# Pairwise products of embeddings and a tower of three layers: table gathers in short rows between the products, and another split of the reductions

## What is computed

```python
e = jnp.stack([tbl_0[ids[:, 0]], ..., tbl_39[ids[:, 39]]], axis=1)   # 512 x 40 x 64
p = e[:, rowidx]          # first of each pair i < j
q = e[:, colidx]          # second of each pair
z = jnp.einsum('bie,fie,bif->bi', p, param, q)                        # 512 x 780
h = jnp.concatenate([z, dense_ctx], axis=1)                           # 512 x 796
h = jnp.maximum(h @ W_top1 + b_top1, 0.0)                             # 512
h = jnp.maximum(h @ W_top2 + b_top2, 0.0)                             # 256
y = h @ W_top3                                                        # 512 x 1
```

## Time and profile before

| | us |
|---|---|
| median of 3 runs | 548.67 |
| lowest and highest | 548.06, 549.01 |
| the profiled run | 548.24 |
| its span | 546.4 |
| TensorE matmuls busy | 322.2 |
| VectorE busy | 258.1 |
| ScalarE busy | 255.2 |
| GpSimd busy | 185.2 |

### The profile page before, as it was taken

One profiled execution on the slowest core, in us unless ns is written; L12 is line 12 of the kernel. 1 busy time (PEld: TensorE's weight loads), 2 busy tenths in 40 slices (PEclk: granted clock), 3 DMA queues, 4 the chain that ended last, 5 costly groups with the idle time before them and its releaser, 6 DMA issues.

```text
span 546.4 us, 7416 instructions
## 1 busy us (share of the span) xinstructions
PE 322.2 (59%) x2318; PEld 165.8 (30%) x2318; DVE 258.1 (47%) x262; ACT 255.2 (47%) x1961; POOL 185.2 (34%) x192
## 2 busy tenths in 40 slices
PE   0402000220003200299999999899779999999988
PEld 0201000000001000155455544454454344444645
DVE  0000000000000000389899988855437999998590
ACT  1000000000002100389999969734687999995632
POOL 6777777777777760000000000000001122232030
PEclk9998555565555755599999999999889999999999
DMA  2221111211112110174324220032124242420000
GB/s 59 46 50 30 26 26 26 55 26 26 26 25 62 26 26 1 39 268 124 125 89 148 88 95 10 11 92 76 46 95 173 95 143 79 172 95 1 1 2 0
DMA packets 12937, 35.60 MB, mean 65 GB/s; under 512 B 4705, under 2 KB 5985, under 8 KB 11618
## 3 DMA queue, kind: packets, MB, share of 16 engines
q1 hardware_dynamic: 7778, 29.88, 16.4%
q0 software_dynamic: 5120, 5.25, 5.0%
HBM read 35.12 MB, written 0.00 MB: 64 GB/s over the span
## 4 chain that ended last, share of the span: by engine, by line
PE 34%; another core or an unknown queue 24%; issue 19%; ACT 13%; DVE 8%; POOL 1%; DMA 1%; DVEq 0%
ACT prod L658 11%; PE upsum L537 9%; PE upsum L532 7%; DVE prod L622 6%; PE zbank L489 6%; PE abank L444 5%; PE abank L423 1%; DVE z L596 1%; POOL emb L396 1%; PE upsum L501 1%; ACT xT L637 1%; PE upsum L505 1%; PE abank L469 1%; PE upsum L573 1%
## 5 line engine op out<-in xcount | busy, mean ns | idle before, releaser
L658 ACT ACTIVATE prod<-prod 128x64 f32<-128x64 f32 x944 | 227.0, 250 | 8.1 <-issue 7.2
L658 ACT ACTIVATION_READ_ACCUMULATOR prod<-prod 128x1 f32 x944 | 185.3, 196 | 7.7 <-issue 7.7
L396 POOL DMA_INDIRECT emb<-tbl,rows_id x160 | 151.5, 947 | 50.2 <-issue 48.5
L622 DVE TENSOR_TENSOR prod<-upsum,emb 128x1024 f32<-128x1024 f32 x98 | 116.8, 1220 | 107.1 <-remote 68.5
L537 PE MATMUL upsum<-w,xT 64*128 64x512 f32 x392 | 106.0, 641 | 102.3 <-issue 59.1
L405 POOL TENSOR_TENSOR prod<-prod 128x512 f32<-128x512 f32 x26 | 32.9, 1271 | 290.4 <-DVE prod L622 290.4
L622 DVE TENSOR_TENSOR prod<-upsum,xT 128x1024 f32<-128x1024 f32 x82 | 97.7, 1219 | 67.2 <-remote 40.0
L637 ACT ACTIVATE xT<-abank 128x256 f32<-128x256 f32 x40 | 15.1, 378 | 220.1 <-remote 129.3
L532 PE MATMUL upsum<-xT,w 64*128 64x256 f32 x656 | 88.3, 397 | 4.9 <-DVE prod L622 2.6
L537 PEld LDWEIGHTS upsum<-w,xT 64*128 64x128 f32 x392 | 33.8, 191 | 140.3 <-issue 81.2
L532 PEld LDWEIGHTS upsum<-xT,w 64*128 64x128 f32 x656 | 60.3, 190 | 35.9 <-issue 16.8
(11 more groups left out here) (46 smaller groups left out, 132.0 us busy)
## 6 DMA issues: line engine op xcount, KB each, us to landing
w<-W_top SPq DMA_DIRECT2D x2, 1792.0 KB, 8.2
emb<-tbl,rows_id POOLq DMA_INDIRECT x160
w<-param SPq DMA_DIRECT2D x2, 1248.0 KB
w<-param SPq DMA_DIRECT2D x2, 1152.0 KB
w<-param SPq DMA_DIRECT2D x2, 1120.0 KB
w<-param SPq DMA_DIRECT2D x2, 1024.0 KB
w<-param SPq DMA_DIRECT2D x2, 992.0 KB
w<-param SPq DMA_DIRECT2D x2, 896.0 KB
```

Source lines behind the costliest of these rows:

```text
L396: pool.indirect_dma_start(emb[:, c, f, :], None, tables[f], bass.IndirectOffsetOnAxis(ap=rows_id[:, c, f:f + 1].bitcast(U32), axis=0),).th ...
L622: dve.tensor_tensor(to.rearrange("p (h q) -> p h q", h=2), t[:], f.broadcast_to([P, 2, BANK]), ALU.mult).then_inc(multiplied, 1)
L658: last = act.activation(ring[:, x * E:(x + 1) * E], ring[:, x * E:(x + 1) * E], ACT.Copy, accum_out=z_view(u)[:, x:x + 1])
```

## The change

Four things change.

1. GpSimd issues the gathers of the first 10 stretches of half 0 (40 DMAs) at the start, eight at a time: ahead of stretches 2, 4, 6 and 8 it waits until all DMAs of the stretch before have landed (`gathered[0][n - 1]`).
2. The other 120 gathers are placed between the halvings, four per stretch. A stretch's gathers stand at 20 units before its first unit, for half 1's first 10 stretches at unit 22 + 6n. Ahead of each four GpSimd waits until all units before that place are multiplied.
3. The shares: H units are dealt from unit 14 on with 0.25 (before: from unit 112 on with 0.22 and 0.3), V units only up to there. The letters of all 200 units are then T 68, S 62, H 48, V 2, C 20; before T 82, S 59, H 26, V 13, C 20. Of units 0 to 79 26 are T, 27 S, 16 H, 2 V and 9 C.
4. VectorE reduces an H unit 5 units later (H_LAG 3 to 5).

The cuts of the groups of sums follow from the letters: half 0 has 3 turned and 4 flat groups, before 4 and 3. The four parts of layer 1 of half 0 stand at units 105, 108, 111 and 115, before at 104, 107, 111 and 115.

```diff
-H_LAG = 3
+H_LAG = 5
...
+GATHER_FIRST, GATHER_AHEAD, GATHER_OTHER, GATHER_STEP = 10, 20, 22, 6
...
-SHARES = [(0, 0.58, 0.32, 0.1, 0.0), (112, 0.4, 0.3, 0.08, 0.22), (130, 0.4, 0.3, 0.0, 0.3)]
+SHARES = [(0, 0.55, 0.35, 0.1, 0.0), (14, 0.42, 0.33, 0.0, 0.25)]
...
-        return max(u + {"S": S_LAG + 5, "V": V_LAG + 3, "H": H_LAG + 3}[units[u]["by"]] for u in members(s, g))
+        return max(u + {"S": S_LAG + 5, "V": V_LAG + 3, "H": H_LAG + 2}[units[u]["by"]] for u in members(s, g))
...
+    gather_at = {}
+    for q in range(NQ):
+        s, n = stretches[q]["s"], stretches[q]["n"]
+        if s == 0 and n >= GATHER_FIRST or s == 1:
+            at = stretches[q]["first"] - GATHER_AHEAD
+            if s == 1 and n < GATHER_FIRST:
+                at = GATHER_OTHER + GATHER_STEP * n
+            assert at <= stretches[q]["first"] - GATHER_AHEAD
+            gather_at.setdefault(max(at, 0), []).append((s, n))
...
-            for s in range(HALVES):
-                for n in range(NC):
-                    for f in (2 * n, 2 * n + 1):
-                        for c in range(s * PER, (s + 1) * PER):
-                            pool.indirect_dma_start(
-                                emb[:, c, f, :], None, tables[f],
-                                bass.IndirectOffsetOnAxis(ap=rows_id[:, c, f:f + 1].bitcast(U32), axis=0),
-                            ).then_inc(gathered[s][n], 16)
+
+            def gather(s, n):
+                for f in (2 * n, 2 * n + 1):
+                    for c in range(s * PER, (s + 1) * PER):
+                        pool.indirect_dma_start(
+                            emb[:, c, f, :], None, tables[f],
+                            bass.IndirectOffsetOnAxis(ap=rows_id[:, c, f:f + 1].bitcast(U32), axis=0),
+                        ).then_inc(gathered[s][n], 16)
+
+            for n in range(GATHER_FIRST):
+                if n >= 2 and n % 2 == 0:
+
+                    pool.wait_ge(gathered[0][n - 1], 16 * 2 * PER)
+                gather(0, n)
             for u in range(NU):
+                for s, n in gather_at.get(u, []):
+
+                    if u:
+                        pool.wait_ge(multiplied, u)
+                    gather(s, n)
                 if units[u]["by"] == "H":
```

## The result

| | before | changed kernel |
|---|---|---|
| median of 4 runs each | 548.47 | 442.10 |
| lowest and highest | 548.06, 549.01 | 440.98, 442.79 |
| ratio, 95% interval | | 0.8058, 0.8039 to 0.8077 |
| span of the profiled run | 546.4 | 439.2 |

The likeliest value, 399 us, was that of case A ("the stall is gone"). The measured time lies where case B put it ("the stall comes back in parts", 420 to 470 us).

What follows compares the result with a forecast made beforehand. Signals delayed by the 160-gather row bound the start; after the change GpSimd's issue does, to unit 81. Span 546.4 - 153.9 + 2 (clock) + 2 (halvings) = 396.5, plus 1.8 and 0.4: 399 us; range 382 to 460, 8 in 10.

Steps and rivals of the forecast that it cites:

- case A: Whole kernel, the forecast itself: the stall at the start is gone, 385 to 420 us; chance 0.62.
- case B: Gather rows from 49 us on, starting with one of 16: the stall comes back in parts, 420 to 470 us; chance 0.20.
- That the long row of gathers is the stall, and that cutting it is the gain: First 228 us: 160 gathers in one row delay other engines' signals; cutting the row gains 153.9 us at unit 81.
- Debt of 0.15 us a gather: Gather rows: something takes 1.40 us per gather, fed each 1.25; eight owe 1.2 us, which a 1.5 us wait clears.
- GpSimd the bound up to unit 81: Start to unit 81: GpSimd runs without a pause; 116 gathers, 16 halvings and four pauses put unit 81 at 175.7 us.
- The 16 halvings' 20.8 us: GpSimd's first-half halvings at 1.30 us each: 20.8 us on the path while GpSimd is the bound.
- Four pauses at 1.5: First 40 gathers, issued eight at a time: GpSimd's four waits for landing cost 1.5 us each, 6.0 us.
- Rival C: Any gather in flight delays signals, not only long rows: slower than before, about 573 us; chance 0.07.
- From unit 81 on: Units 81 to the end: 216.8 us as before, plus 2 us for halvings late behind four gathers.
- The clock: Up to unit 81: TensorE's lower clock level behind idle gaps adds 2 us to the path, bounds 0 and 10.

Runs made afterwards that it cites:

- changed up to unit 112, nothing held (other chip): Changed kernel with shares T 0.4, S 0.3, H 0.3 from unit 112 on, run where the kernel before took 367.6 us: 396.0 us, ratio 1.077.
- before with spacer: Kernel before with a GpSimd memset of 128 x 256 behind each of its 160 gathers: 506.7 us, ratio 0.9225, where the kernel before took 548.3.
- spacer of 512: Kernel before with a GpSimd memset of 128 x 512 behind each gather, on the chip where the kernel before took 367.6 us: 402.4 us, one run.
- the changed kernel with the spacer: Changed kernel with a memset of 128 x 256 behind each gather, where the kernel before took 367.6 us: 429.0 us, ratio 1.168.

## Why the prediction was right in its range and 43 us off in its value

All terms side by side, in us of the span:

| | unit 81 | from unit 81 on | span |
|---|---|---|---|
| before | 329.6 | 216.8 | 546.4 |
| forecast | 175.7 + 2 | 216.8 + 2 | 396.5 |
| changed kernel | 210.3 | 228.9 | 439.2 |
| changed up to unit 112, nothing held (other chip) | 175.0 | 219.6 | 394.6 |
| old split, pacing only | 225.8 | 225.6 | 451.4 |
| new split, no pacing | 330.5 | 227.3 | 557.8 |
| new split, no gathers | 141.2 | 225.2 | 366.4 |
| old split, plain DMAs | 132.0 | 217.4 | 349.4 |
| before with spacer | 291.3 | 216.7 | 508.0 |
| before with pauses every eight | 286.3 | 217.9 | 504.2 |
| changed, rows of four | 215.2 | 230.8 | 446.0 |

- **That the long row of gathers is the stall, and that cutting it is the gain:** right, and shown from both sides: the new split alone gives no gain, the pacing alone 96 us, and without indirect gathers the stall is gone.
- **Debt of 0.15 us a gather, "so the debt is cleared each time, and I take the stall as gone":** this is the step that failed, and with 33 us in the first part it is most of the miss (210.3 - 177.7). The 1.40 us per gather came from two ends of one stretch, as the text says, and did not fit the text's own row between them: 17 gathers owe 2.6 us by it, and the delay was 14.3. The spacer and the pauses show late signals where it leaves no debt, and in the changed kernel the fourth pause of 1.78 us did not end waits that began at 45.4. The first 45 us went as forecast: four pauses of 1.7 to 2.0 us, and no wait named "remote".
- **GpSimd the bound up to unit 81, 116 x 1.25 + 16 x 1.30 + ...:** the sum is right where nothing is held (175.0 measured), wrong here, since it presumes that the products always run ahead of GpSimd. Here GpSimd waited 32.8 us for them. The 16 halvings' 20.8 us lie on the path only in the first case; here they lay in time that was free anyway. The Trainium skill (GPSIMD Engine Reference, section 4.1, engine selection) puts elementwise adds on VectorE. The pacing with the new split took 442 us, with the old one, which has no halvings in the first half, 452; so with the hold the measurement does not bear the rule out, though no run moves the halvings alone. No run tried the paced kernel without them on the other chip.
- **Four pauses at 1.5:** 1.71, 1.99, 1.73 and 1.78, 7.2 us in place of 6.0. The Trainium skill (DMA: Bandwidth & Descriptors, the anatomy of one DMA on the SWDGE path) gives a fixed cost of some 2.0 us for such a DMA. An estimate from it, counted from the end of issue, is 8.0; the trace lies between.
- **Rival B:** named the right place (the row of 16 from 49 us on) and the right brake ("each delay makes GpSimd wait for products"), at 420 to 470 us with a chance of 0.20. The range held 442 us because it took in B, not because the forecast's path was right. B should have been the larger part: its own evidence, 17 gathers with 14.3 us of delay, was as good as the evidence for A, and the row of 16 stood in the order.
- **Rival C,** "if a row of eight already delays a signal": rows of eight do delay signals. That it gave no slower kernel is because products do run in the gaps that the pacing leaves: GpSimd, waiting for late products, issues nothing. With pauses of only some 2 us between eights and no waits for products it is 494 to 506 us, still under the 548 of one long row.
- **From unit 81 on:** +12.1 where +2 was taken, the second miss, 10 us. Most of it belongs to the new split: the spans of that part are 225 to 231 us in all kernels with it unchanged, also without gathers (225.2) and without pacing (227.3), and 217 to 218 in those with the old split and no waits for products. (With the spacer of 512 it is 239, since its gathers still run then.) Changing the shares from unit 112 on (less S, more H) gave 219.6, on the other chip; there the changed kernel with the spacer took 227.0. By stages 81, 99, 128, 180, 199 and end:

| | 81 to 99 | to 128 | to 180 | to 199 | to the end |
|---|---|---|---|---|---|
| before | 27.9 | 71.3 | 68.4 | 34.7 | 14.6 |
| changed kernel | 25.4 | 71.7 | 72.2 | 40.5 | 19.2 |
| new split, no gathers | 25.0 | 72.0 | 68.4 | 40.8 | 19.1 |
| old split, pacing only | 27.8 | 71.7 | 76.8 | 34.7 | 14.6 |

The change of halves is as it was. The 10 us behind unit 180 stand there without gathers too, so these are the split's. Part of them is one wait of TensorE for ScalarE's copy, 4.0 us, the first row below; all six traces with the unchanged new split have it, those with the old split or with other shares from unit 112 on don't at that place. The 3.8 us from 128 to 180 are gone without gathers, and the old split with pacing alone, 8.8 us over before (225.6 against 216.8), loses 8.4 of them in that stage: both go with the gathers that now stand there. How the gathers cost them isn't shown; little is held there (4.4 us with pacing alone).

That wait, and in the tail one for its sums (PE, after):

```profile
387.56 0.66 PE L463 MATMUL abank<-ident,z 128*128 128x128 f32 x2 [3.98 <-ACT xT L662]
...
421.89 0.42 PE L463 MATMUL abank<-ident,z 128*96 128x128 f32 x2 [3.63 <-DVE z L621]
```

In the second row TensorE stands idle for 3.63 us until VectorE has reduced the last H unit, 0.7 us behind the last product; before it stood 0.18 us at that place. That wait stands with the other shares from unit 112 on as well (3.6 us), and not with pacing alone, whose H_LAG is 3 (0.2 us). That the longer lags make it was not tried by itself.

- **The clock:** the mean granted clock up to unit 81 was 0.84, against the 0.98 of the busy stage before. Its 2 us were not measured apart. On the other chip, with 0.91, the sum without them was met within 1 us.

## What to carry to other kernels

A wait whose releaser the trace calls "remote", with the producer long done, is a late signal and not late data; see what another engine is issuing in a row at that time, and replace its form (here indirect by plain DMAs) for one run, before a rate is fitted to it. A row of such instructions should be broken where consumers need their signals, but each pause costs the issuing engine its landing time: here rows of 8 to 16 (442 us) beat both one row of 160 (548) and rows of four (449). And time the kernel before on more than one chip: here the change is worth a fifth of the time where gathers hold signals, while on the chip where they don't a kernel that differs from it only in the shares from unit 112 on lost 8%.

## What the runs showed of the hardware

- 160 indirect gathers of 128 rows in one row on GpSimd (0.95 us and a gap of 0.30) held single signals of TensorE to ScalarE and VectorE for up to 67 us, and again in the new split without pacing. 160 plain DMAs of the same size, 0.53 us each, held none. What part of the core holds them stays open, and so does whether it is the signal or the waiting instruction that is late. The Trainium skill (SBUF — State Buffer, "Who interferes with whom") says that a DMA never contends with a compute engine, and that where a VectorE instruction seems to stall a DMA, GpSimd was kept from building its descriptors. Here it is not that: the gathers kept their 0.95 us, and VectorE stood idle while it was held.
- Within such a row not every signal is held. Single ScalarE instructions of one unit, which wait for nothing, come up to 1.9 us late behind the one before in a row's later gathers (62 gaps, 30.8 us in the whole run of the changed kernel; with rows of four 12 gaps, 4.9 us). The traces without gathers, with plain DMAs and of the chip with 368 us have none. So not only instructions that wait for a signal are late.
- The same kernel took 548 us on three chips and 368 us on a fourth; the kernels traced there issue a gather in the same 0.95 us.
- A gather's pause, from the end of its issue to its landing, was 1.7 to 1.8 us in three of the changed kernel's four, with the 16 DMA engines about 0.1 busy, and 2.0 in the fourth at 0.58. The longest, 5.3 us (pauses every eight) and 4.5 us (rows of four), stand beside parameter loads at 0.48 and 0.53.
